# Two routes for a residual in a fused recurrent and mixture-of-experts kernel: transposes with copies, or float32 identity matmuls in the bank of the second biases

## The reference, cut to what matters

```python
x  = x  + _L0_ffn_ref(_L0_cond_ref(x, cond, w_cond), w_gate, w_up, w_down)   # first layer: gives "x1" in the kernel
x  = x1 + _L1_ffn_ref(_L1_cond_ref(x1, cond, Wx, Wh, b), router_w, w1, b1, w2, b2)

def _L1_cond_ref(x, h0, Wx, Wh, b):          # 128 steps, 16 sequences, 128 features
    xw = einsum('ntd,dh->nth', x, Wx) + b
    step: h = tanh(xw_t + h @ Wh)            # strictly one after the other

def _L1_ffn_ref(h, router_w, w1, b1, w2, b2):   # 8 experts, 512 inner features, best 2 of 8
    logits = h @ router_w.T;  top 2;  softmax over the two
    y_e = gelu(h @ w1[e].T + b1[e]) @ w2[e].T + b2[e]
    return sum over the two chosen experts of weight_e * y_e
```

## Time and profile before

| | |
|---|---|
| median of three runs | 293.2 us |
| profiled execution | 293.86 us |
| its span, first to last instruction | 292.1 us |
| TensorE (PE) busy | 258.1 us, 88% of the span |
| VectorE (DVE) busy | 257.5 us, 88% |
| ScalarE (ACT) busy | 218.5 us, 75% |
| GpSimd (POOL) busy | 91.9 us, 31% |
| granted TensorE clock, mean | 0.953 of full speed |

### The profile page before, as it was taken

How to read it: one execution, slowest core, us unless ns; L and a number is a source line. 1 busy time by engine, 2 the same in 40 slices (tenths; PEclk the granted TensorE clock), 3 DMA queues, 4 the chain that set the end, 5 groups by cost and what they waited for, 6 DMA issues and landing times.

```text
span 292.1 us, 7662 instructions
## 1 busy us (share of the span) xinstructions
PE 258.1 (88%) x2828; PEld 196.1 (67%) x2828; DVE 257.5 (88%) x638; ACT 218.5 (75%) x510; POOL 91.9 (31%) x181
## 2 busy tenths in 40 slices
PE   4999850039999999999999999999999999999994
PEld 3843450016866889888888676767677777778774
DVE  4899999989999999979988799778799988899885
ACT  5487899998742677777777777787678777788992
POOL 3539999250036413113212213333211232201000
PEclk9999957558999999999999999999999999999999
DMA  6992343001400000000000000000001000001001
GB/s 172 325 333 47 72 95 72 15 0 36 92 18 2 1 2 2 3 0 21 2 0 3 2 5 25 2 2 3 1 2 38 3 0 2 3 2 37 0 2 29
DMA packets 24041, 10.77 MB, mean 37 GB/s; under 512 B 13355, under 2 KB 22982, under 8 KB 24006
## 3 DMA queue, kind: packets, MB, share of 16 engines
q1 hardware_dynamic: 23470, 10.05, 13.7%
q10 hardware_dynamic: 536, 0.26, 0.3%
HBM read 6.11 MB, written 1.05 MB: 25 GB/s over the span
## 4 chain that ended last, share of the span: by engine, by line
PE 69%; DVE 24%; DMA 3%; issue 2%; ACT 1%; POOL 0%; SPq 0%; DVEq 0%
PE bank L998 68%; DVE peak L723 6%; DVE peak L805 4%; DVE big L829 3%; DVE big L841 3%; DMA wn<-in_w_gate 2%; DVE q L795 1%; DVE big L810 1%; DMA y_sb<-in_cond 1%; PE bank L1124 1%; DVE ws L750 1%; DVE big L836 1%; DVE big L849 1%; DVE big L977 0%; DVE pkm L712 0%
## 5 line engine op out<-in xcount | busy, mean ns | idle before, releaser
L998 PE MATMUL bank<-big,wt 128*128 128x384 f16 (+2 forms) x480 | 123.1, 336 | 0.0
L998 PE MATMUL bank<-wt,big 128*128 128x128 f16 (+1 forms) x1536 | 110.8, 219 | 0.2 <-DVE big L977 0.2
L998 PEld LDWEIGHTS bank<-wt,big 128*128 128x128 f16 x1536 | 98.2, 97 | 15.9 <-DVE big L977 0.5
L977 DVE TENSOR_TENSOR big<-big 128x384 f16<-128x384 f32 (+2 forms) x160 | 93.1, 587 | 17.7 <-ACT big L679 13.2
L677 ACT ACTIVATE big<-bank,miscT 128x384 f32<-128x384 f32 (+2 forms) x160 | 96.5, 604 | 10.3 <-PE bank L998 9.4
L998 PEld LDWEIGHTS bank<-big,wt 128*128 128x128 f16 (+1 forms) x480 | 44.8, 107 | 3.8 <-issue 0.2
L459 POOL TENSOR_TENSOR big<-q,big 128x16 f16<-128x16 f32 x56 | 23.5, 419 | 66.6 <-ACT q L666 66.6
L973 DVE CAST big<-big 128x512 f16<-128x512 f32 (+2 forms) x104 | 38.7, 372 | 4.0 <-ACT big L677 3.5
L932 DVE SCALAR_TENSOR_TENSOR wyT<-bank,gates,wyT 128x128 f32<-128x128 f32 x128 | 39.7, 343 | 0.3 <-issue 0.2
L679 ACT ACTIVATE big<-bank,miscT 128x384 f16<-128x384 f32 (+2 forms) x56 | 33.1, 592 | 0.0
L665 ACT ACTIVATE big<-bank,miscT 128x16 f16<-128x16 f32 x56 | 15.4, 276 | 18.1 <-PE bank L998 17.9
(11 more groups left out here) (177 smaller groups left out, 386.1 us busy)
## 6 DMA issues: line engine op xcount, KB each, us to landing
wnat<-in_w SPq DMA_DIRECT2D x8, 512.0 KB, 7.6
x_sb<-in_x SPq DMA_DIRECT2D x4, 256.0 KB, 4.1
out_block<-wyT SPq DMA_DIRECT2D x15, 64.0 KB
wn<-in_w_gate ACTq DMA_DIRECT2D x1, 192.0 KB, 5.4
wn<-in_w_up SPq DMA_DIRECT2D x1, 192.0 KB, 5.5
wn<-in_w_down SPq DMA_DIRECT2D x1, 192.0 KB, 5.5
b_in<-in_b SPq DMA_DIRECT2D x12, 4.0 KB
wt<-wyT SPq DMA_TRANSPOSE x8, 3.0
```

The costliest lines, as they stand in the source:

```text
L977: V.tensor_tensor(g_lo[:, par, f, 0:w], g32[:, f, 0:w], g_hi[:, par, f, 0:w], ALU.subtract).then_inc(g_lo_done, 1)
L998: return nc.tensor.matmul(o, l, r, start=start, stop=stop, skip_group_check=True)
```

## The change

The residual no longer enters `acc` before the experts. `transpose_x1` and the four copies are gone, with their semaphores. In `mix_b2(c)` the product of gates and `b2` is followed, in the same bank 3, by one float32 matmul for each tile of the chunk: the stationary operand is the tile of `x1`, the moving one a float32 identity scaled by 2^18, so that it adds the transposed tile, scaled as the biases are. `add_b2` is unchanged and brings both to `acc`. The first expert now writes `acc` (`tensor_scalar`) instead of adding to it, which needs the expert's number when the program is written, so that all five chunks are written out (`UNROLLED = 5`). The remaining first step comes after `input_part`.

```diff
-UNROLLED = 4
+UNROLLED = 5
-ACC_SCALAR = (2, 3)
-LATE = NK - len(ACC_SCALAR)
+LATE = 0
+        ident_up = sb("ident_up", [P, P])
@@ gpsimd, among the constants
+            G.tensor_scalar(ident_up[:, :], ident[:, :], GATE_UP, 0.0, ALU.mult, ALU.add).then_inc(consts, 1)
@@ scalar, after the first steps
-            for k in ACC_SCALAR:
-                act.wait_ge(x1T_mm, k + 1)
-                A(acc[:, 4 * k:4 * k + 4, :].rearrange("p j h -> p (j h)"), banks[ACC_BANKS[k]][:, :],
-                  ACT.Copy).then_inc(acc_s, 1)
@@ vector, after make_x1(CH - 1) and its wait for the transposed weights
-            for k in range(ACC_SCALAR[0]):
-                dve.wait_ge(x1T_mm, k + 1)
-                V.tensor_copy(acc[:, 4 * k:4 * k + 4, :].rearrange("p j h -> p (j h)"),
-                              banks[ACC_BANKS[k]][:, :]).then_inc(added, 1)
             split_x1(CH - 2)
-            dve.wait_ge(acc_s, len(ACC_SCALAR))
@@ add_gated
-                V.scalar_tensor_tensor(a, ps_y[par][:, P * j:P * (j + 1)], g, a, ALU.mult, ALU.add).then_inc(added, 1)
+                y = ps_y[par][:, P * j:P * (j + 1)]
+                if e == 0:
+                    V.tensor_scalar(a, y, g, None, ALU.mult).then_inc(added, 1)
+                else:
+                    V.scalar_tensor_tensor(a, y, g, a, ALU.mult, ALU.add).then_inc(added, 1)
@@ tensor, after the last down matmul
-            transpose_x1(0)
-            for r in range(step, FIRST_STEPS):
-                first_step(r)
-            transpose_x1(1)
             pe.wait_ge(w_lo_s, W_CHUNKS - W_POOL)
             pe.wait_ge(x1_lo_done, 2)
             input_part(FIRST_STEPS, RNN_FROM[1])
-            transpose_x1(2)
-            transpose_x1(3)
+            for r in range(step, FIRST_STEPS):
+                first_step(r)
@@ mix_b2
-                mm(banks[3][:, 0:WIDTHS[c]], gateT[:, :], b2_diag[:, 0:WIDTHS[c]], True).then_inc(b2_mm, 1)
+                pe.wait_ge(consts, 5)
+                pe.wait_ge(x1_done, c + 1)
+                mm(banks[3][:, 0:WIDTHS[c]], gateT[:, :], b2_diag[:, 0:WIDTHS[c]], True)
+                for j in range(TILES[c]):
+                    tile = slice(START[c] + P * j, START[c] + P * (j + 1))
+                    last = mm(banks[3][:, P * j:P * (j + 1)], x1[:, tile], ident_up[:, :], False)
+                last.then_inc(b2_mm, 1)
@@ pair on TensorE
-                    if c == 0 and first and s in (0, 2):
-                        pe.wait_ge(added, 1 + s // 2)
-                    if c == 0 and first and s == NF:
-                        pe.wait_ge(acc_s, len(ACC_SCALAR))
+                    if c == 0 and first and s < 2:
+                        pe.wait_ge(x1_done, DOWN_BANKS.index(NF + s) + 1)
```

More of the change, by code:

```diff
@@ L160, in program @@
         wt_t = [sem(f"wt_t{i}") for i in range(2)]
-        acc_s, w_hi_s, w_lo_mm, w_lo_s = sems("acc_s w_hi_s w_lo_mm w_lo_s")
+        w_hi_s, w_lo_mm, w_lo_s = sems("w_hi_s w_lo_mm w_lo_s")
         consts, cond_T, cond_sb, norm_in, norm_mm, norm_sb, root_done, norm_done = sems(
@@ L171, in program @@
             "gu_mm gu_sb gateq upq sig_done sig_round sig_16 g2_done g2q p_done oq o_hi_done o_lo_done o_lo_p")
-        down_mm, x1_done, x1_hi_done, x1_lo_done, x1_hi_p, x1_lo_p, x1T_mm = sems(
-            "down_mm x1_done x1_hi_done x1_lo_done x1_hi_p x1_lo_p x1T_mm")
+        down_mm, x1_done, x1_hi_done, x1_lo_done, x1_hi_p, x1_lo_p = sems(
+            "down_mm x1_done x1_hi_done x1_lo_done x1_hi_p x1_lo_p")
         nat_done, small_w, rw_done = sems("nat_done small_w rw_done")
@@ L191, in program @@
         DOWN_BANKS = [1, 2, 3, 4, 5]
-        ACC_BANKS = [4, 6, 1, 2]
         GU_BANKS = [5, 6, 0, 1, 2]
@@ L252, in chunks @@
                 if c < UNROLLED:
-                    for e2 in range(1, E // 2):
+                    for e2 in range(1, E // 2 - (c == CH - 1)):
                         pair(c, e2, True)
@@ L1116, in first_step @@
                 mm(ps_first[:, B * r:B * (r + 1)], w_h32, state, False).then_inc(rnn_mm, 1)
[L1120 to L1126, removed]
             step = 0
```

## The result

The changed kernel takes 296.69 us (median of 4, 296.56 to 297.2) against 293.1 us before (four runs, with one more than above): ratio 1.012, 95% interval 1.0108 to 1.0132, 3.6 us slower. Run once more beside the later experiments it took 296.95 us against 293.31, ratio 1.0117 (1.0102 to 1.0133). The forecast was 296.3 us, in a range of 295.3 to 297.6. The profiled execution took 297.2 us, with a span of 295.4.

What follows compares the result with a forecast made beforehand. TensorE was taken to bound the kernel from 105.9 us on. Matmuls +3.5 us, passage -0.4, small edits -0 to 0.1 make +3.1 on 293.2: 296.3 us, range 295.3 to 297.6.

Steps and rivals of the forecast that it cites:

- What bounds: From 105.9 us on TensorE is busy almost without a break, so whatever is added to its program adds to the time.
- Rival 3: Matmuls of `mix_b2` absorbed in the first pairs, where VectorE would set the pace: 292.5 us in total; 6%.
- Price of the groups: Sixteen float32 matmuls in five `mix_b2` calls, 0.218 us each, add 3.5 us on TensorE; 3.3 to 4.4 us.
- the two readings of the same shape: Price of a float32 tile: 0.218 us at the transposes' pace, taken, or 0.27 us beside a float16 matmul, perhaps an uncovered load.
- rival 1: Float32 pairs in `mix_b2` cost 0.275 us as beside the float16 matmul: +4.1 us, 297.3 us in total; 15%.
- Passage: From 95.33 us to chunk 0's start at 98.11, removed transposes and copies give 0.1 to 0.9 us; taken as 0.4.
- The gain behind the start: After chunk 0 starts, ScalarE has no copies before the second layer's first tanh: some 0.2 us, within the passage's 0.4.
- the sign that I had named: In the changed trace, the first long TensorE piece of the chain starts near 105.5 us.
- Small edits: Cheaper first expert worth 0 to 0.1 us; writing out the last chunk and the constant on GpSimd cost nothing.
- `add_b2` was covered: VectorE's `add_b2` waits up to 0.9 us for the longer group, but in the first chunk comes three slots later.

Runs made afterwards that it cites:

- e3: The kernel before with the sixteen float32 matmuls added in `mix_b2`, everything else as it was: 297.34 us, ratio 1.0133.
- e1: The changed kernel with the sixteen float32 matmuls of `mix_b2` left out, so the residual is missing: 293.25 us, ratio 0.9993.
- e7: The changed kernel with VectorE's split of `x1`'s fourth chunk held back until GpSimd has written the first states' halves: 297.04 us, ratio 1.0127.
- e2: The changed kernel with six unused float16 matmuls on TensorE filling its wait in the passage: 296.54 us, ratio 1.0115.
- e5: The changed kernel with each float32 matmul of `mix_b2` replaced by two float16 ones, of the halves of `x1`: 294.74 us, ratio 1.0046.
- e4: The kernel before with only the last chunk written out instead of looped: 293.36 us, ratio 1.0005.
- e6: The changed kernel without the sixteen float32 matmuls and with six unused matmuls filling the wait in the passage: 292.88 us, ratio 0.9984.

## Why the prediction was right

**What bounds.** Right. Added work on TensorE came out in full: e3 shows it on the unchanged kernel, e1 the reverse. Rival 3, which had the matmuls absorbed, is refuted in all five calls by the starts. (The two long pieces of the earlier trace rows contain all five calls, the first at 131.28; the prediction counted four.)

**Price of the groups.** 3.5 us forecast, 3.57 measured. Of the two readings of the same shape, the pace of the transposes (0.218 us a tile) was right and the 0.27 us beside a float16 matmul was not. The reason given, a load that isn't covered there and is here, fits the traces: the load starts 0.06 us ahead of the matmul there (80.14 and 80.20) and 0.11 us ahead here (130.71 and 130.82). As a mechanism rival 1 is out. Its total isn't: the traces of before and after differ by 4.2 us where it had 4.1, by other terms.

**Passage.** The start of chunk 0 was forecast 0.3 us earlier with VectorE blocking GpSimd, 0.65 us without; it is 0.25 us earlier, with the blocking, and e7, 0.58 us earlier, shows that blocking to be the reason. What was blocked was GpSimd's subtraction (0.63 us); the cast, on which the prediction had reasoned, kept its 0.24 us. The gain behind the start was taken as 0.1 us of the total; with the clock kept it is 0.4 us (e2: 24.54 against 24.93). So with the clock kept the passage was worth 0.65 us, within the bounds of 0.1 to 0.9.

**The steps that were missing.** I followed when TensorE would start, and never wrote down that until then it would have nothing to do (95.67 to 97.04 in the changed trace). Behind that wait the clock went to half for 3.4 us in both traces of the changed kernel and in e1, not in e5, and it cost 0.9 us where it did: in these traces a gain of 0.65 us became a loss of 0.25. At half clock TensorE has no wait for VectorE left in chunk 0, so the sign that I had named, a long piece of the chain that starts near 105.5, didn't appear; it starts at 97.04 (in e2, with the clock kept, at 104.76). The second missing term is the 0.35 us of chunk 2: I had reckoned with VectorE blocking GpSimd in the passage and not in the recurrence.

**How near the number was.** The traces differ by 3.57 + 0.25 + 0.35 = 4.2 us, the medians by 3.6, against a forecast of +3.1. So the forecast is low by 0.5 by the medians and by 1.1 by the traces. Their difference isn't explained: the sums leave the first layer out, and how often the clock falls is unknown. By the medians of e3 and of the changed kernel the groups cost 4.1 us and the passage gives 0.4 to 0.65; then the 0.4 us for the passage was right, and only the groups' term was too small. That the median came within 0.5 us of the forecast owes something to luck: two costs were left out, and in the traces they add up to 1.25 us (0.9 and 0.35). The direction was never in doubt.

**Small edits.** The written-out loop is worth nothing that shows (e4). VectorE's plain multiplication for the first expert took 0.34 to 0.35 us, no less than the fused one, not the 292 ns I read off one instruction near the start; behind TensorE it makes no difference. `add_b2` was covered: VectorE came to it at 133.34, and the group was over at 131.27. The constant on GpSimd (0.30 us) shows no trace.

## What to carry to other kernels

Work moved from a passage onto the engine that bounds the long stage costs its full start-to-start time; price it by the pace of back-to-back rows of the same shape, not by one row with a different neighbour. Where a queue gets shorter, write down what the engine waits for next and for how long: here a hole of 1.4 us on TensorE, with the fall of the clock behind it, gave back more than the removed work had been worth in the executions whose traces show it. And GpSimd's idle time isn't free where VectorE is late: one addition held VectorE for a microsecond. The reverse holds too: three of GpSimd's small subtractions, held up by VectorE's, cost TensorE 0.35 us.

## What the hardware showed beside that

- A TensorE wait of 1.37 us behind a nearly full queue was followed, a microsecond after it ended, by 3.4 us at half clock in three traces (changed twice, e1), and by nothing in a fourth (e5, the same wait). With unused matmuls in the hole (e2, e6) and with a wait of 1.05 us (e7) the clock stayed. What decides between them is open.
- At full clock, in an otherwise full queue, a 128x128 tile added through an identity costs TensorE 0.223 us in float32 and 0.112 us as two float16 halves.
- GpSimd's 128x16 subtraction takes 0.21 us by itself and 0.71 us when VectorE's 128x512 subtraction (0.69 us) starts with it.
